# Layer 1 of a four-layer graph network: ScalarE writes zeros into a unit's PSUM slots and TensorE opens the banks with shorter products

## What is computed

```python
edge_index = jnp.stack([src, dst])
x = _layernorm(x + _L0_gnn_ref(x, W_t, W_u, b_u, src, dst))                    # mean of h[dst] over src
x = _layernorm(x + _L1_gnn_ref(x, eps, edge_index))                            # the layer of this change
x = _layernorm(x + _L2_gnn_ref(x, w, w, src, dst, ...))                        # weighted sum into dst
x = _layernorm(x + _L3_gnn_ref(x, edge_attr, glob, ..., src, dst))             # mish messages into dst

def _L1_gnn_ref(x, eps, edge_index):
    row, col = (edge_index[0], edge_index[1])
    deg = jax.ops.segment_sum(jnp.ones(col.shape), col, num_segments=n)
    deg_inv_sqrt = jnp.where(deg > 0, jax.lax.rsqrt(deg), 0.0)
    norm = deg_inv_sqrt[row] * deg_inv_sqrt[col]
    agg = jax.ops.segment_sum(norm[:, None] * x[col], row, num_segments=n)
    return agg + (1.0 + eps[0]) * x
```

## Time and profile before

| | us |
|---|---|
| timed runs, median of 3 | 8724.96 |
| timed runs, lowest and highest | 8724.23, 8733.42 |
| profiled execution, first to last instruction | 11115.3 |
| granted TensorE clock over it, mean | 0.757 |
| share of the span busy: PE, DVE, ACT, POOL | 63%, 48%, 30%, 56% |

### The profile page before, as it was taken

One profiled execution on the slowest core, in us unless ns is written; L12 is line 12 of the kernel. 1 busy time (PEld: TensorE's weight loads), 2 busy tenths in 40 slices (PEclk: granted clock), 3 DMA queues, 4 the chain that ended last, 5 costly groups with the idle time before them and its releaser, 6 DMA issues.

```text
span 11115.3 us, 153275 instructions
## 1 busy us (share of the span) xinstructions
PE 7035.5 (63%) x41943; PEld 5709.6 (51%) x41944; DVE 5383.7 (48%) x10966; ACT 3359.4 (30%) x7561; POOL 6201.5 (56%) x6523
## 2 busy tenths in 40 slices
PE   4677777667757888888844444444445666666666
PEld 2555555555646777777733333333334555555555
DVE  6676666666664666655551222222223444444444
ACT  4334234322030000000021222222224665555564
POOL 2555555555525555555546666666655665556564
PEclk6878778877678999999975666656667777777777
DMA  1111111111121111111121111111112333233332
GB/s 28 37 39 40 39 40 39 41 38 39 35 82 50 41 41 42 39 42 42 38 74 47 52 50 52 53 52 51 52 50 78 89 88 87 81 86 85 87 88 63
DMA packets 575360, 611.55 MB, mean 55 GB/s; under 512 B 114414, under 2 KB 472474, under 8 KB 574618
## 3 DMA queue, kind: packets, MB, share of 16 engines
q0 software_dynamic: 203776, 417.74, 14.4%
q1 hardware_dynamic: 294120, 145.77, 4.5%
q10 hardware_dynamic: 76722, 38.13, 1.2%
HBM read 562.68 MB, written 38.51 MB: 54 GB/s over the span
## 4 chain that ended last, share of the span: by engine, by line
PE 33%; another core or an unknown queue 23%; DVE 21%; issue 19%; ACT 3%; DVEq 1%; POOL 0%; DMA 0%; ACTq 0%; SPq 0%; POOLq 0%
PE ps L1906 10%; PE ps L2177 7%; DVE oh L1918 5%; DVE acc L1936 3%; PE ps L1817 3%; PE ps L2234 2%; PE ps L1771 2%; DVE oneh L1411 1%; PE ps L1772 1%; DVE acc L2195 1%; DVE posi L1394 1%; PE ps L1452 1%; PE ps L1689 1%; PE ps L1776 1%
## 5 line engine op out<-in xcount | busy, mean ns | idle before, releaser
L1996 POOL DMA_INDIRECT M<-in_x,ixb x1664 | 1638.9, 985 | 1165.9 <-issue 693.3
L2043 POOL DMA_INDIRECT M<-t,ixb x1664 | 1618.1, 972 | 1024.0 <-issue 606.6
L2043 POOL DMA_INDIRECT M<-x,ixb x1664 | 1586.8, 954 | 884.2 <-issue 578.4
L2177 PE MATMUL ps<-M,oh 128*128 x7056 | 1402.4, 353 | 962.8 <-issue 814.4
L1996 POOL DMA_INDIRECT M_any<-t,ixb x1376 | 1305.2, 949 | 1104.7 <-issue 579.7
L2177 PEld LDWEIGHTS ps<-M,oh 128*128 128x128 f32 x7056 | 1214.1, 247 | 1271.7 <-issue 1199.5
L2195 DVE TENSOR_TENSOR acc<-acc,ps 128x1024 f32 x294 | 359.3, 1222 | 3087.3 <-remote 1844.6
L1936 DVE TENSOR_TENSOR acc<-acc,ps 128x774 f32 (+1 forms) x988 | 942.8, 954 | 1699.5 <-remote 945.9
L1435 ACT ACTIVATE oht<-oneh,ot 128x128 f16<-128x128 f16 x3264 | 969.7, 387 | 1597.3 <-DVE oneh L1411 1438.3
L1906 PE MATMUL ps<-M,oh 128*128 x5928 | 1121.0, 338 | 282.9 <-issue 235.5
L1906 PEld LDWEIGHTS ps<-M,oh 128*128 128x128 f32 x5928 | 1008.2, 238 | 510.0 <-issue 443.3
(11 more groups left out here) (305 smaller groups left out, 9727.7 us busy)
## 6 DMA issues: line engine op xcount, KB each, us to landing
er<-in_edge_attr SPq DMA_DIRECT2D x414, 256.0 KB
M<-in_x,ixb POOLq DMA_INDIRECT x1664
M<-x,ixb POOLq DMA_INDIRECT x1664
M<-t,ixb POOLq DMA_INDIRECT x1664
M_any<-t,ixb POOLq DMA_INDIRECT x1376
x<-lay SPq DMA_DIRECT2D x48, 256.0 KB, 2.3
part<-x ACTq DMA_DIRECT2D x48, 256.0 KB
lay<-in_x SPq DMA_DIRECT2D x24, 256.0 KB, 4.1
```

Of the source, the lines that this page charges most:

```text
L1996: e.indirect_dma_start(M1[:, m1_slot(s, t), :] if layer else M[:, t % RING, 0:P], None, table[0:rows, :], bass.IndirectOffsetOnAxis(ap=ixb ...
L2043: e.indirect_dma_start(M2[:, t % RING, :], None, table[:, :], bass.IndirectOffsetOnAxis(ap=ixb[:, t:t + 1], axis=0)).then_inc(s_g[n % 16], 16)
L2177: ins = e.matmul(ps_flat[:, bass.ds(slot * P, P)], oh[:, j, :], tile_at(M2, tile, P), start=False, stop=False)
```

## The change

In layer 1 a new `clear_act` on ScalarE writes zeros over the unit's six slots (768 columns from `ps_flat[h * 1024]`) and adds to a new semaphore `s_clr`. It waits for what TensorE's opening waited for: `s_add` of unit u-2, and `s_ot` where that unit carried a row. TensorE waits for `s_clr` and opens each of the two banks with a product of 128 columns. ScalarE's copies of expanded tiles are put between the clears: a tile whose last product lies in unit v (`made_in`) is copied behind the clear of unit v+1. Before layer 1, ScalarE also waits for VectorE's last node operations of layer 0. Layer 0 keeps its opening.

```diff
+            def made_in(x):
+                w = WIN[x // XT + 1]
+                return -int(-(due(x) + (2 * PERIOD - 2 * US) * (w - 1) / w) // 1) // US
+
+            def clear_act(e, u):
+                h = u % 2
+                e.wait_ge(s_add, ST0[1] + max(u - 1, 0) * US + 1)
+                if u - 2 in ROW_UNIT:
+                    e.wait_ge(s_ot, ROW_UNIT[u - 2] + 1)
+                e.activation(ps_flat[:, h * 1024:h * 1024 + US * P], zwin[:, 0:1].to_broadcast([P, US * P]), ACT.Copy).then_inc(s_clr, 1)
+
             def expand_act(e):
                 load_window(e, 1)
-                for x in range(X_ALL):
-                    s, i = x // XT + 1, x % XT
-                    e.wait_ge(s_xp, x + 1)
...
+                x = 0
+                for u in range(U_ALL):
+                    clear_act(e, u)
+                    while x < X_ALL and made_in(x) < u:
+                        s, i = x // XT + 1, x % XT
+                        e.wait_ge(s_xp, x + 1)
...
+                        e.activation(M1[:, RG + i, :], ps[:, 4 + x % 2, 0:P], ACT.Copy).then_inc(s_xc, 1)
+                        x += 1
...
-                    e.wait_ge(s_add, max(1, ST0[layer] + (u0 + h - 1) * US + 1))
-                    if layer and u0 + h - 2 in ROW_UNIT:
-                        e.wait_ge(s_ot, ROW_UNIT[u0 + h - 2] + 1)
-                    clear_pe(e, b0, *((2 * PITCH + W1C, 2 * PITCH + W1C + 1) if layer == 0 else (4 * P, 3 * P)))
+                    if layer == 0:
+                        e.wait_ge(s_add, max(1, (u0 + h - 1) * US + 1))
+                        clear_pe(e, b0, 2 * PITCH + W1C, 2 * PITCH + W1C + 1)
+                    else:
+                        e.wait_ge(s_clr, u0 + h + 1)
+                        clear_pe(e, b0, P, P)
...
                 stores_done(e, tal)
+                for t in tal:
+                    wait(e, t[2].at())
                 expand_act(e)
```

More of the change, by code:

```diff
@@ L127, in graph_layers @@
         s_raw, s_src, s_wld, s_wgt = (sem(n) for n in ("s_raw", "s_src", "s_wld", "s_wgt"))
-        s_gx, s_ot, s_xp, s_xc, s_xw, s_map = (sem(n) for n in ("s_gx", "s_ot", "s_xp", "s_xc", "s_xw", "s_map"))
+        s_gx, s_ot, s_xp, s_xc, s_xw, s_map, s_clr = (sem(n) for n in ("s_gx", "s_ot", "s_xp", "s_xc", "s_xw", "s_map", "s_clr"))
         s_dum, s_dum_v, s_dum_a, s_dum_s = (sem(n) for n in ("s_dum", "s_dum_v", "s_dum_a", "s_dum_s"))
@@ L1835, in load_window @@
                     e.dma_start(xw[:, b % XR:b % XR + n, :], t1[b * P:(b + n) * P, :].rearrange("(i p) f -> p i f", p=P)).then_inc(s_xw, 16)
+            def made_in(x):
[7 more added lines that the diff above has]
+                e.activation(ps_flat[:, h * 1024:h * 1024 + US * P], zwin[:, 0:1].to_broadcast([P, US * P]), ACT.Copy).then_inc(s_clr, 1)
             def expand_act(e):
                 load_window(e, 1)
-                for x in range(X_ALL):
-                    s, i = x // XT + 1, x % XT
-                    e.wait_ge(s_xp, x + 1)
[L1842 to L1846, removed]
+                x = 0
[4 more added lines that the diff above has]
+                        e.wait_ge(s_xp, x + 1)
+                        if i == 0 and s + 1 < SUP:
+                            load_window(e, s + 1)
+                        last = min(X_TILES[i] + NB - 1, K - 1)
+                        e.wait_ge(s_st, ST0[1] + (s - 1) * KP + (last // US + 1) * US)
+                        e.activation(M1[:, RG + i, :], ps[:, 4 + x % 2, 0:P], ACT.Copy).then_inc(s_xc, 1)
+                        x += 1
+                assert x == X_ALL
             def window_rows(e, s):
```

## The result

| | before | after |
|---|---|---|
| timed runs, median of 20 each, us | 8721.24 | 8710.06 |
| lowest to highest | 8713.85 to 8733.42 | 8705.29 to 8713.8 |
| ratio after / before, 95% interval | | 0.9987, 0.9981 to 0.9993 |

The change makes the kernel faster by 11 us, 0.13%: a real difference, but within the 0.2% that the forecast called no change. TensorE's two openings became as short as expected, but most of the time that they left was spent again right behind them, on TensorE itself.

A forecast was written before the change was run, and what follows sets the result against it. GpSimd's gathers were taken to bound the kernel: 7960 us of gathers plus 704 without any gave 8664, near the timed 8725. With GpSimd's path unchanged and some 5 us to be had, the forecast was 8720, range 8640 to 8765.

The forecast's parts named there:

- GpSimd's path: Layer 1 from TensorE's first unit: 9 + 1640 for 1312 gathers + some 8 = 1657 us, setting the end.
- The sum of 8664: Whole kernel: 6368 gathers at 1.25 us, 7960, plus 704 without gathers; within 61 us of the timed median.
- TensorE's path: Layer 1: 1583 us without waits, about 1667 with 33 + 51 of waits; a tie with GpSimd.
- (1): TensorE's layer 1 openings: 0.38 to 0.12 us a unit, saving 128 us of TensorE's time, bounds 79 to 163.
- (2): ScalarE's write of 128 x 768 into PSUM, layer 1: 0.82 us each, 405 us in all, hidden.
- (3): Layer 1's wait for ScalarE's write: round trip 6.63 us per two units against GpSimd's 6.84, 0.2 to spare.
- (4): ScalarE's copies of expanded tiles, queued behind its waits: up to one unit later, costing nothing.
- (5): Start of layer 1: ScalarE waits for layer 0's stores, then writes 0.82 us; +1 us on the path.
- A: Faster rival: TensorE binds layer 1 in timed runs too; 8665 us, at most down to 8597; chance 0.36.
- B: Slower rival: the round trip through ScalarE becomes layer 1's bound; +47, 8772 us; chance 0.12.
- C: Slower rival: TensorE, waiting more in layer 1, falls to half clock rate; +45, 8770 us; chance 0.06.
- D: Rival: short openings cost their upper bound, saving 79 us instead of 128; time stays; no chance given.

The follow-up runs named there:

- b0: Kernel before plus masks on register values that change no value, one more TensorE register instruction per 12 steps: 8730.53 us, ratio 1.0006.
- e1_short: Against b0: TensorE's layer 1 openings at 128 columns, old waits, no ScalarE zeros, other slots not cleared: 8720.07 us, ratio 0.9994.
- e2_wait: Against a0: TensorE's openings long again (512 and 384 columns), ScalarE's zeros and the wait for them kept: 8741.53 us, ratio 1.0019.
- a0: Kernel after the change plus the same masks as b0: 8728.03 us, ratio 1.0000.
- e8: Against b0: two shorter register instructions per layer 1 step, bank offset put into the table by VectorE: 11225.89 us, ratio 0.9971 of before.
- e7: Against a0: two shorter register instructions per layer 1 step, bank offset put into the table by VectorE: 11254.83 us, ratio 1.0002 of before.
- e4: Against b0: a layer 1 step's two addresses from two register instructions, not three: 11064.28 us, ratio 0.9945 of before.
- e3: Against a0: two register instructions per layer 1 step, not three, one a chain of six operations: 11135.83 us, ratio 1.0009 of before.
- a0_again: The kernel of a0 unchanged, run again as control in a later group: 11291.79 us, ratio 1.0028 of before.
- S: Not a run but a theory: TensorE's queue with its register instructions binds layer 1, and the long openings lay beside them.
- e5: Against a0: four register instructions per layer 1 step instead of three, the slot by a second AND: 11232.79 us, ratio 1.0102 of before.

## Why the prediction came out as it did

**The outcome.** Forecast 8720 and no change; measured 8710.06 against 8721.24. The time was right, the reason was not.

**What bounds the kernel: the step that failed.** "In the timed runs GpSimd gathers almost without a break, in layer 1 as elsewhere." It doesn't in layer 1: with TensorE at work the full ring held it for 65 us in the kernel after, 89 in b0. GpSimd's path from TensorE's first unit was put at 1657 us; its last gather started 4253 - 2537 = 1716 us after it, and TensorE's last opening 1757. The sum of 8664 came near the timed median since two errors partly cancelled. The times in which no gather can run, taken from the stretched profile, were 136 + 114 + 122 + 62 + 89 = 523; in the profile after they are 136 + 56 + 119 + 41 + 82 = 434. They were 89 too large. Inside the layers, from first to last gather and beyond 1.25 us for each, some 163 us were lost in layer 0, 100 in layer 1, 7 in layer 2 and 46 in layer 3, together 316, where the sum had 181. Layer 1's 100 are as many as the forecast had, but it put all of them before TensorE's start, and 65 came behind it. A profile that is 27% longer than the timed runs gave durations of single instructions well, but no sum of gaps.

**TensorE's path.** 1583 us of matmuls was a good count: if every spacing is taken at the lowest fifth of its kind, the starts of b0's layer 1 add up to 1554. The 84 us allowed for waits were far too few: b0 needed 1782. Of the 228 us above 1554, 77 stand between step passes and 47 between expansion passes, the rest in smaller items. A term that the forecast left out is the queue, three register instructions a step, which no view lists; how much of the 228 is the queue's, the runs do not separate. That the openings' saving lies for the larger part beside this queue is the likely reason why 128 us of TensorE's time gave 11; it is argued from the traces of b0 and e1_short. What e1_short shows by its time is that the saving was not there to be lost to the new wait.

**(1) The opening.** Right. 3001.78 and 3001.84 are 0.06 apart, the median over the layer is 0.056 and 0.060 to the next matmul, so 0.116 for the pair against 0.12. The estimate that the prediction worked out from the formula of the Trainium skill, page "TensorE: Matmul & The Clock Gate", section "Back-to-back issue gap", 0.112, agrees.

**(2) ScalarE's write.** Right: 0.813 us against 0.82, 402 us in all, hidden for the most part.

**(3) The new wait.** Its size was right in kind: openings waited 45 us for ScalarE, in 20 units, and the wait alone cost 11 us (b0 to e2_wait). "This round trip is what is late next" is not what the first condition shows, where VectorE waits 339 us for TensorE. In the second condition it is: the 0.34 us from close to addition was a prompt handover, and the late one beside it in the earlier trace rows, 4.09 us of waiting, was set aside as the profiled execution's doing. The groups over 11000 us show that timed runs can have it too.

**(4) The copies**: no wait for them shows among TensorE's in layer 1. **(5) The start** can't be told from nothing: TensorE's first opening of layer 1 is at 2530.3 us in a0 and in b0.

**The rivals.** A had the right side, TensorE's, and the wrong cap: the gain stopped at 11 us, long before GpSimd's pace, at which 60 us were to be had; TensorE's own queue is the likely cap. B did not happen at 8725 us; in the runs over 11000 the sign is B's, 29 and 72 us slower where only the change differs (e8 to e7, e4 to e3), though not through the 0.33 us a pair that B counted. C did not happen at 8725 us, where the granted clock of layer 1 is 0.97. In the second condition C's sign is there beside B's: 0.87 in e7_sub_after and 0.88 in a0_again, against 0.92 in e8_sub_before and in the profile before. D did not: the openings cost what was forecast. Of the signs named, gathers 1.25 us apart in unbroken runs is the one that failed, and it was the one on which the forecast stood.

**What stays open.** S rests on the traces of the first group and on the masks' 16 us. e5 and e7 show that the number of queue instructions counts in the second condition, where these instructions are themselves stretched. No time in the first condition shows what a shorter queue would bring there, and how much of the spent time is the weight loads' or the lower clock's is only estimated. No version beat both kernels: after is best where before takes 8725 us; where it takes over 11000, e4_two_before and e8_sub_before are (0.9945 and 0.9971 of before), and neither was run in the first condition.

## What to carry to other kernels

A shorter matmul need not shorten the kernel: what its columns covered can come into the open behind it. Where matmuls take addresses from registers, count the register instructions between them before counting columns. When a profile's span is far from the timed runs, take durations of single instructions from it, and never the sum of its gaps as a proof of what binds. Look there whether handovers come late, and how long the lower clock lasts, before a change adds a wait to every round trip.

## What was not expected of the hardware

- A simple register instruction on TensorE's queue took 0.032 to 0.036 us and a gap of some 0.06 (first group). A fused one took longer with other operations in it: 0.090 us for two chains of three with a shift, 0.143 for two of three with a subtraction (e7_sub_after), 0.176 for one of six (e3_two_after).
- From TensorE's close to VectorE's addition it took 0.34 us in a0 and 2.5 us in the median, 5.6 at the 95th percentile, in a0_again, with the same kernel; the kernel's time was 29% longer.
- In the same long runs TensorE's stream stops by itself: passes of expansion that follow at 0.11 us were over 0.3 us apart 153 times, against 10.
